# Two attention blocks over 16 images: first half of the keys one gap later, and other places for pieces in the first and last full round

## The reference

```python
# block 0: 4 heads of 32 channels, 1024 queries and 1024 keys
_x = group_norm(x, 32 groups) * gn_scale + gn_bias
q, k, v = Wq/Wk/Wv applied to _x, plus biases          # (B, 4, 32, 1024)
weights = softmax(q.k / sqrt(128))                      # per head, 1024 x 1024
h = weights . v;  h = Wp h + bp;  x = (x + h) / sqrt(2)
# block 1: one head of 128 channels
h = group_norm(x, 8 groups) * gn_w + gn_b
q, k, v = split(h . qkv_w + qkv_b)
attn = softmax(q.k / sqrt(128));  out = attn . v
x = out . proj_w + proj_b + x
```

## Time and profile before

| | |
|---|---|
| median of 3 runs | 1640.89 us (1640.61 to 1641.0) |
| the profiled execution, its own time | 1639.49 us |
| its span, first to last instruction | 1637.7 us |
| mean granted TensorE clock | 0.987 |
| busy share of the span | TensorE 96%, GpSimd 73%, VectorE 70%, ScalarE 67% |

### The profile page before, as it was taken

The page is one execution under the profiler, slowest core; times in us unless marked ns, Lnnn a source line. Parts: engine busy times, 40 slices in busy tenths (PEclk is TensorE's granted clock), DMA queues, the critical chain, the costliest instruction groups (busy, mean ns, idle before and its releaser), DMA issues.

```text
span 1637.7 us, 26098 instructions
## 1 busy us (share of the span) xinstructions
PE 1576.2 (96%) x9511; PEld 1094.9 (67%) x9511; DVE 1144.1 (70%) x1961; ACT 1095.7 (67%) x1858; POOL 1189.6 (73%) x563
## 2 busy tenths in 40 slices
PE   7888999999999999999999999999999999999998
PEld 5434667667667766766676766767667676765567
DVE  7567776777777777777777777677777767765242
ACT  1445777676677776767777677777767776765655
POOL 2687977788587787868789687778868777887610
PEclk7889999999999999999999999999999999999999
DMA  6504041140413205041231414114141410400000
GB/s 180 153 20 122 20 120 50 40 110 20 129 40 90 59 33 136 21 129 40 75 75 33 118 38 129 40 54 96 33 117 40 118 51 26 111 20 7 7 7 20
DMA packets 47662, 111.72 MB, mean 68 GB/s; under 512 B 5808, under 2 KB 6448, under 8 KB 47536
## 3 DMA queue, kind: packets, MB, share of 16 engines
q1 hardware_dynamic: 47248, 109.86, 24.3%
q10 hardware_dynamic: 288, 0.20, 0.0%
HBM read 67.84 MB, written 41.94 MB: 67 GB/s over the span
## 4 chain that ended last, share of the span: by engine, by line
PE 83%; DVE 6%; DMA 5%; ACT 3%; issue 2%; SPq 0%; POOL 0%; ACTq 0%; POOLq 0%
PE bank L1073 13%; PE scores L1041 13%; PE acc L998 13%; PE scores L980 12%; PE scores L1028 6%; PE scores L1020 4%; DVE halfmax L859 4%; PE scores L1021 3%; PE bank L1090 3%; PE scores L1022 3%; DMA k_stack<-parts_dram 3%; PE bank L1108 2%; PE bank L1112 2%; DMA parts_dram<-k_lo 1%; PE acc L1080 1%
## 5 line engine op out<-in xcount | busy, mean ns | idle before, releaser
L627 POOL TENSOR_TENSOR sum<-sum,probs 128x1024 f32<-128x1024 f32 x444 | 1043.2, 2381 | 280.8 <-PE acc L998 268.6
L859 DVE TENSOR_REDUCE halfmax<-bank 128x1 f32<-128x512 f32 x968 | 631.8, 680 | 208.5 <-PE bank L1073 208.2
L675 ACT ACTIVATE probs<-scores 128x512 f32<-128x512 f32 x896 | 515.6, 600 | 204.4 <-PE scores L980 198.6
L980 PE MATMUL scores<-q_stack,k_stack 97*128 97x512 f32 x1024 | 436.2, 437 | 3.2 <-issue 1.4
L1073 PE MATMUL bank<-k_stack,q_stack 96*128 96x512 f32 x952 | 384.0, 425 | 13.7 <-DVE halfmax L859 6.3
L1073 PEld LDWEIGHTS bank<-k_stack,q_stack 96*128 96x128 f32 x952 | 176.2, 190 | 148.5 <-DVE halfmax L859 65.2
L1041 PEld LDWEIGHTS scores<-v,turned 128*128 128x128 f32 x1952 | 251.1, 192 | 30.5 <-ACT turned L695 14.0
L1041 PE MATMUL scores<-v,turned 128*128 128x128 f32 x1952 | 258.2, 277 | 4.4 <-ACT turned L695 3.8
L980 PEld LDWEIGHTS scores<-q_stack,k_stack 97*128 97x128 f32 x1024 | 194.1, 191 | 58.3 <-issue 27.4
L998 PE MATMUL acc<-probs,v 128*32 128x512 f32 x1792 | 220.4, 603 | 0.0
L898 DVE TENSOR_REDUCE negmax<-scores 128x1 f32<-128x1024 f32 x128 | 156.7, 1224 | 68.8 <-PE scores L1022 66.5
(11 more groups left out here) (121 smaller groups left out, 1600.9 us busy)
## 6 DMA issues: line engine op xcount, KB each, us to landing
q_stack<-parts_dram SPq DMA_DIRECT2D x96, 256.0 KB, 5.2
k_stack<-parts_dram SPq DMA_DIRECT2D x96, 256.0 KB, 7.6
xin<-x_dram SPq DMA_DIRECT2D x16, 512.0 KB, 3.5
x<-x_dram SPq DMA_DIRECT2D x16, 512.0 KB, 3.5
parts_dram<-q_hi SPq DMA_DIRECT2D x16, 512.0 KB, 2.6
parts_dram<-q_lo SPq DMA_DIRECT2D x16, 512.0 KB, 3.5
parts_dram<-k_hi SPq DMA_DIRECT2D x16, 512.0 KB, 2.6
parts_dram<-k_lo SPq DMA_DIRECT2D x16, 512.0 KB, 3.6
```

The source lines that it names most:

```text
L627: pool.tensor_tensor(total, total, probs[:, ring_slot(i, half, kt), 2 * two:2 * two + 2, :], ALU.add).then_inc(added[two], 1)
L675: act.activation(dst, score_bank(i, index), ACT.Exp).then_inc(exp_done, 1)
L859: dve.tensor_reduce(halfmax[:, h, t, half:half + 1], banks[p][:, :], AX.X, ALU.max).then_inc(bank_free[p][VE], 1)
L980: pe.matmul(score_bank(i, index), ks[0:SPLIT + 1, i % 2, h, tile(kt)], qs[0:SPLIT + 1, q_half(i, half), h, :], start=True, stop=True).then ...
```

## The change

1. In every round from 1 to 14, `k0` of the first half moves from gap 8 to gap 9 on all three engines. In gap 9 it stands behind `score1` of a block 1 tile on TensorE and ahead of a maximum.
2. Round 0: `q0` of both halves moves from gaps 7 and 8 to gap 5; `k0` from gaps 8 and 10 to gaps 6 and 7 (VectorE: gap 8 for both); `v0` of image 1 from gaps 14 and 21 to 11 and 20; the value pair of gap 43 is split, its first step (the first of the second half) in gap 39, its second in gap 43.
3. Round 15: the tile pieces of block 1 take the distances of `ROUND` and its order inside a gap (`turn` 3 gaps after the start of the tile instead of 4, `pv1a` and `pv1b` in gaps 5 and 6 instead of both in 7, `exp1` in gap 1 or 2); `out` of the first half moves from gap 16 to 13; the value pair of gap 43 is split as in round 0; the very first value step moves from gap 5 to gap 8; `affine1` from gap 30 to 27, `norm1` from 33 to 31. The last pieces of the third tile, which stood in gap 0 of the tail, end in gap 63.

```diff
--- before.py
+++ after.py
@@ -97,7 +97,7 @@
     ("hi0", 0, 2, None, GAPS + 0, None),
     ("q0", 0, 2, GAPS + 7, GAPS + 7, GAPS + 7),
     ("q0", 1, 2, GAPS + 8, GAPS + 8, GAPS + 8),
-    ("k0", 0, 2, GAPS + 8, GAPS + 8, GAPS + 8),
+    ("k0", 0, 2, GAPS + 9, GAPS + 9, GAPS + 9),
     ("k0", 1, 2, GAPS + 10, GAPS + 10, GAPS + 10),
     ("v0", 0, 2, GAPS + 14, GAPS + 14, None),
     ("v0", 1, 2, GAPS + 21, GAPS + 21, None),
@@ -159,27 +159,23 @@
 HEAD_GAPS = 13 + FIRST
 FIRST_MAX = [*range(4), *(g for g in range(10, 24) for _ in range(2))]
 
-ROUND_FIRST = [p for p in ROUND if (p[0] not in ("max", "gather", "shift") or p[2]) and p[:3] != ("pv", 0, 0)] + [
-    ("pv_a", 0, 0, 5, None, None), ("pv_b", 0, 0, 11, None, None), ("v0", 1, 0, 1, 1, None)] + [
+EARLY_VALUES = [("pv_a", 0, 0, 5, None, None), ("pv_b", 0, 0, 11, None, None),
+                ("pv_a", 4, 0, 39, None, None), ("pv_b", 4, 0, 43, None, None)]
+EARLY_PAIRS = [("pv", n, 0) for n in (0, 4)]
+FIRST_PROJECTIONS = [
+    ("q0", 0, 1, 5, 5, 5), ("q0", 1, 1, 5, 5, 5), ("k0", 0, 1, 6, 6, 8), ("k0", 1, 1, 7, 7, 8),
+    ("v0", 0, 1, 11, 11, None), ("v0", 1, 1, 20, 20, None),
+]
+ROUND_FIRST = [p for p in ROUND if (p[0] not in ("max", "gather", "shift") or p[2]) and p[:3] not in EARLY_PAIRS
+               and p[:3] not in [q[:3] for q in FIRST_PROJECTIONS]] + EARLY_VALUES + FIRST_PROJECTIONS + [
+    ("v0", 1, 0, 1, 1, None)] + [
     ("max", FIRST + n, 0, g, None, g) for n, g in enumerate(FIRST_MAX)] + [
     ("gather", 1, 0, None, None, 24), ("shift", 1, 0, 25, None, 25)]
 
 
-def end_tile_pieces(t, offset, first):
-    return [("score1", (t, 0), offset, first, None, None), ("score1", (t, 1), offset, first + 1, None, None),
-            ("max1", t, offset, None, None, first + 1), ("exp1", t, offset, None, first + 1, None),
-            ("rinv", t, offset, None, None, first + 3), ("turn", t, offset, first + 4, first + 4, None),
-            ("pv1a", t, offset, first + 7, first + 7, None), ("pv1b", t, offset, first + 7, None, None)]
-
-
-END_AT = {(n % KT, n // KT - 2): TILE_FIRST + TILE_GAPS * n - GAPS for n in range(3, 3 + KT)}
-TILE_PIECES = ("score1", "max1", "exp1", "rinv", "turn", "pv1a", "pv1b")
-
-END_PIECES = [("out", 0, -2, 16, None, 16), ("pv_a", 0, 0, 5, None, None), ("pv_b", 0, 0, 11, None, None),
-              ("affine1", 0, -1, None, None, 30), ("norm1", 0, -1, None, 33, None)]
-ROUND_END = [p for p in ROUND if p[0] not in TILE_PIECES and p[:3] != ("pv", 0, 0)
-             and p[:3] not in [q[:3] for q in END_PIECES]] + END_PIECES
-END_TILES = folded([p for (t, offset), first in END_AT.items() for p in end_tile_pieces(t, offset, first)])
+END_PIECES = [("pv_a", 0, 0, 8, None, None)] + EARLY_VALUES[1:] + [
+    ("affine1", 0, -1, None, None, 27), ("norm1", 0, -1, None, 31, None)]
+ROUND_END = [p for p in ROUND if p[:3] not in EARLY_PAIRS and p[:3] not in [q[:3] for q in END_PIECES]] + END_PIECES
 
 
 DIRECT = 2
@@ -214,8 +210,7 @@
     ("v1", 0, -1, 34, 34, None), ("v1", 1, -1, 34, 34, None),
 ]
 
-LATER = [p for p in END_TILES if p[2] == -2 and tile_of(p) < LAST_TILE]
-ROUND_END += [p for p in END_TILES if p not in LATER]
+LATER = [p for p in folded(BLOCK1) if p[2] == -2 and p[0] != "out" and tile_of(p) < LAST_TILE]
 ROUND_LAST = LATER + [p for p in folded(VALUES) if p[2] == -1] + LAST_CHAIN + LAST_BLOCK1 + [
     ("out", 0, -2, LAST_AT[3, -2] + 11, None, LAST_AT[3, -2] + 11),
     ("out", 1, -2, LAST_AT[KT - 1, -2] + 11, None, LAST_AT[KT - 1, -2] + 11),
```

## The result

The kernel after took 1619.74 us (median of 4 runs, 1618.85 to 1621.17) where the kernel before, on the same chip, took 1640.75 us (1639.36 to 1641.0): a ratio of 0.9875, 95% interval 0.9857 to 0.9892, or 21 us less. A second measurement of the same kernel, on another chip, gave 0.9895 (0.9881 to 0.9908). The prediction was 1624.0 us with a range of 1617 to 1631: the time lies inside, 4.3 us under the forecast.

What follows compares the result with a forecast made beforehand. TensorE, busy 96% of the span, bounds rounds 2 to 14, and latency between engines both ends. Terms 5.2 + 3.6 + 8.0 = 16.8 us off 1639.49 give 1622.7; adjusted to the median, 1624.0 us, range 1617 to 1631.

Steps and rivals of the forecast that it cites:

- Part 1: Rounds 1 to 14, `k0` one gap later: 5.2 us gained, bounds 0 and 12.9.
- The steps on the calm rounds: Rounds without late key loads: 0.92 us wait removed, 0.1 left, 0.3 lost at gap 11's maximum; 0.5 us gained per round.
- where the loads are late: Gap 20, six of rounds 2 to 14: key loads follow the second half's `k_lo`, gaining 0.25 us per round.
- Rival (c): Gap 20's first maximum: key loads land later every round, at 1.5 us more per round 1649 us; chance 0.03.
- Part 2: Round 0, early projections and split value pair: 3.6 us gained, bounds 1.3 and 4.5.
- The split pair: Round 0, value pair of gap 43: the projection's 1.31 us wait for `mix` goes, 0.1 us is paid; gain 1.3.
- The early projections: Round 0 up to gap 24: second `k_lo` 1.2 us earlier plus 1.1 us less VectorE idle time, 2.3 us gained.
- Part 3: Round 15 and the tail: 3.6 us gained in the first 20 gaps, 4.4 behind; 8.0 us, bounds 4 and 11.
- The 7.7 us of work: Round 15's last tiles: TensorE work counted per tile, 14 matmuls, 24 more and a value pair, against 9.32 us taken.
- Rival (a): Gaps 9 to 11 or key loads take over the wait, Part 1 gives 0: 1629 us; chance 0.14 shared with (d).
- (b): Round 15 is bound by a tile's chain also in gaps 0 to 28, Part 3 gives 4: 1628 us; chance 0.12.
- (d): `k0` waits in gap 9 as in gap 8 because `q_lo` is late: 1629 us; chance 0.14 shared with Rival (a).

Runs made afterwards that it cites:

- k0_only: The kernel before with only `k0` moved from gap 8 to gap 9 in rounds 1 to 14: 1629.91 us, ratio 0.9945.
- k0_keys_held: The kernel before with `k0` moved to gap 9, and SyncE starting `k_hi`'s write only when `k_lo` is done too: 1639.96 us, ratio 1.001.
- tiles alone: The kernel before with round 15's new block 1 tile distances, `out`, `affine1` and `norm1`, value steps unmoved: 1633.64 us, ratio 0.9964.
- all: The kernel before with all of the change's round 15 and nothing else: 1628.50 us, ratio 0.9940.
- end_values: The kernel before with only round 15's first value step moved to gap 8 and its gap 43 pair split: 1638.32 us, ratio 0.9996.

## Why the prediction was nearly right

**Part 1, said 5.2 us, is about 8.** The steps on the calm rounds hold: said 0.92 - 0.1 - 0.3 = 0.5, measured 0.59, with the gap 11 wait at 0.25. What failed is "where the loads are late the gain of a round is the 0.25 us by which they start earlier". I had tied both key writes to the second half's `k_lo`. But SyncE writes `k_hi` when both halves of `k_hi` are done, which stood behind the first half's wait, and this write came 0.9 us earlier; the write of `k_lo` behind it then landed 0.6 us sooner after its issue. The loads left 0.96 us earlier, so late rounds gained as calm ones and a little more. With the write held back nothing is left of the 8 us; had it only kept its time, about 4 would be left by the estimate above, near the 5.2 said.

**Rival (c)** was right about the place and wrong in sign. The price per us of landing holds: with the held writes waits stood in 14 rounds, of 0.32 us where the third load landed at 32.0 us of the round and 1.66 where it landed at 33.3. The Trainium skill (DMA: Bandwidth & Descriptors, Issuing engines are not separate DMA queues) has transfers interleave on the same 16 engines. The runs fit it, with a small price: a `k_hi` write issued 1 us before `q_lo`'s landed took 2.7 to 2.8 us instead of 2.6.

**Part 2, said 3.6 us, is 1.4 in like profiles and not to be seen in the time.** The split pair is as counted (said 1.3, is 1.04). The early projections, said 2.3, bring 0.35. The step that failed is the 1.1 us for "VectorE's idle time of 2.00 us before 67.27 ... is replaced by 0.9": those 2.00 us were the work of half a clock, low from 64.6 to 68.0 us in that execution. Of the six profiles with the old order of round 0 the three with a low stretch there have 2.00 us (also `k0_only` and `k0_keys_held`), the three without have 0.89, so at full clock there was nothing to replace. The other 1.2 us (`k_lo` earlier) is 0.92. The bound named there, VectorE's row of maxima sets the end, is nearly what happened.

**Part 3, said 8.0 us, is 7.5 in the profile and 8.0 at equal clock.** Score 20 was said at 28.3 and came at 28.02; the gain behind it was said 4.4 and is 3.6 (1.9 to the last score, 1.7 behind). The 7.7 us of work that I counted for a tile were too few: 9.38 us less one wait of 0.63 with its surcharge leave 8.5. The waits for `oevict` went, as said; those before `pv1a` stayed, at 0.53 and 0.63. I gave the wait at the accumulator in gap 5 to the move, rightly (1.13 us between tiles alone and all), and missed that the split pair in gap 39 can wait for it too; with the new distances it does not.

**Sum.** At equal clock the parts alone are 8.1 + 0.9 + 8.0 = 17.0 us, the whole 17.5, the forecast 16.8. Rival (a) fell with the calm rounds, (b) with the 3.9 us gained by score 20, where it had the tile's chain bind, and 7.5 in all against its 4, (d) with the start of `k0` at 0.23 us. That the sum was this near owes something to two errors of opposite sign, 3 us too little in part 1 and 2 to 3 too much in part 2. That cancelling is luck. The 21 us of the first measurement have some 3 us in them that neither the parts nor the second measurement show. The 1.1 us by which round 0 started earlier are not the change's either: with the head's code the same, that start lay between 42.65 and 43.97 us in ten profiles. What varies there I have not followed.

## What to carry to other kernels

Where a step is moved on one engine, follow every transfer to the instruction that it really waits for: two writes in one queue can hang on different results, and when the first one leaves can decide when the second lands (0.6 us here). Before a wait in a stage with a varying clock is costed, see whether the clock was full there; an idle time beside a half-clock stretch may not exist in the next execution (2.00 us in three profiles here, 0.89 in three). A wait that is filled with other work often has another late result right behind it: look for what is due next on each engine before moving work into it, and move both.

## What the runs showed of the hardware

- One 512 KB write lands 2.6 us after its issue. A second one issued 0.4, 0.8 and 1.4 us behind it lands 4.1, 3.6 and 3.1 to 3.3 us after its own issue (medians), which is 1.6 to 1.9 us behind the first one's landing each time.
- The mean granted clock goes with more than half of this kernel's spread from run to run (correlation -0.77 over 68 runs of before). But for the two behind the long waits of `k0_keys_held`, all stretches at 1.2 GHz between the start of round 0 and the end of the work lie in the first 175 us, at other places from one execution to the next for the same order of work: 64.6 to 68.0 us in before, none between 54.1 and 81.3 in `end_values`. A value pair in one took 3.30 us instead of 1.93. With 4 to 6 runs of each, two kernels 3 us apart could not be told from each other by the time, while rounds 2 to 14 took 1246.8 to 1247.4 us in three profiles with the new `k0` and 1253.4 to 1257.1 in six with the old one.
